# Two transformer layers in one kernel: dt made ahead of the x-projection by a merged weight, and attention's parts stored first

## The reference

```
xz = u @ m_in_w.T;  xc, z = split(xz)
xc = silu(causal_conv4(xc) + conv_b)
x_dbl = xc @ xproj_w.T                        # 8 columns for dt, 16 for B, 16 for C
dt = softplus(x_dbl[..., :8] @ dt_w.T + dt_b) # 256 channels
Bm, Cm = x_dbl[..., 8:24], x_dbl[..., 24:]
h = exp(dt * A) * h + dt * Bm * xc            # a scan over 512 steps, 16 states per channel
y = (sum over states of h * Cm + xc * Dp) * silu(z)
return y @ m_out_w.T
```

## Time and profile before

| | us |
|---|---|
| median of 3 timed runs | 2080.14 (2078.58 to 2081.39) |
| the profiled execution, its own time | 2059.48 |
| its span in the trace | 2057.8 |
| TensorE busy in the span | 1652.5 (80%) |
| VectorE busy | 1350.7 (66%) |
| ScalarE busy | 1003.5 (49%) |
| GpSimd busy | 995.8 (48%) |

### The profile page before, as it was taken

The page is one execution under the profiler, slowest core; times in us unless marked ns, Lnnn a source line. Parts: engine busy times, 40 slices in busy tenths (PEclk is TensorE's granted clock), DMA queues, the critical chain, the costliest instruction groups (busy, mean ns, idle before and its releaser), DMA issues. The chain is left out here.

```text
span 2057.8 us, 23202 instructions
## 1 busy us (share of the span) xinstructions
PE 1652.5 (80%) x7221; PEld 730.4 (35%) x7221; DVE 1350.7 (66%) x1527; ACT 1003.5 (49%) x1638; POOL 995.8 (48%) x524
## 2 busy tenths in 40 slices
PE   7767788888888888875855957698888889879998
PEld 5221222222222222211454744354444445633333
DVE  3079999999999999999552123566565655384444
ACT  3566666676666776674122523154444445441111
POOL 1169999999999999998441153011111000040000
PEclk8878888888888888877957966599999989989999
DMA  3044344434443433333003221422233330100001
GB/s 140 2 104 104 92 103 103 103 93 103 103 103 95 101 90 88 89 87 91 16 30 103 82 67 50 116 59 56 49 77 79 79 79 4 46 0 0 0 0 41
DMA packets 78636, 145.41 MB, mean 71 GB/s; under 512 B 10214, under 2 KB 40782, under 8 KB 76854
## 3 DMA queue, kind: packets, MB, share of 16 engines
q1 hardware_dynamic: 75350, 134.98, 25.8%
q0 software_dynamic: 3216, 9.51, 1.4%
HBM read 87.27 MB, written 23.53 MB: 54 GB/s over the span
## 5 line engine op out<-in xcount | busy, mean ns | idle before, releaser
L574 POOL TENSOR_TENSOR PR<-H,CS 128x1024 f32<-128x1024 f32 x256 | 599.4, 2359 | 75.1 <-DVE H L550 52.8
L550 DVE TENSOR_TENSOR_SCAN H<-DA,X 128x1024 f32<-128x1024 f32 x192 | 431.1, 2273 | 0.0
L456 PE MATMUL psY<-PR,fold 128*64 128x512 f32 x1024 | 341.0, 766 | 4.9 <-POOL PR L574 4.9
L538 DVE TENSOR_TENSOR X<-DU,psB 128x1024 f32<-128x1024 f32 x192 | 235.8, 1228 | 72.9 <-DMA DU<-ab 56.8
L526 ACT ACTIVATE DA<-DT,negA 128x511 f32<-128x511 f32 x384 | 247.6, 709 | 7.3 <-DMA DT<-W 6.4
L1278 ACT ACTIVATE a_PT<-a_psS 128x512 f32<-128x512 f32 x320 | 181.3, 601 | 138.5 <-PE a_psS L1182 134.6
L1325 DVE TENSOR_REDUCE a_MX<-a_psM 128x1 f32<-128x384 f32 (+3 forms) x352 | 205.0, 635 | 47.0 <-PE a_psM L1197 45.5
L1196 PE MATMUL a_psM<-a_kst,a_qst 72*128 72x512 bf16 (+3 forms) x512 | 147.4, 336 | 28.0 <-DMA a_kst<-scratch_k 17.5
L550 DVE TENSOR_TENSOR_SCAN H<-X,XS 128x1024 f32<-128x1024 f32 x64 | 146.2, 2284 | 30.2 <-ACT X L526 30.2
L585 POOL TENSOR_TENSOR XS<-DU,BS 128x1024 f32<-128x1024 f32 x64 | 151.0, 2360 | 0.0
L436 PE MATMUL psB<-ST,sel 96*128 96x512 bf16 x128 | 60.8, 475 | 106.4 <-DVE X L538 106.4
(11 more groups left out here) (258 smaller groups left out, 2733.0 us busy)
## 6 DMA issues: line engine op xcount, KB each, us to landing
CS<-c_rows SPq DMA_DIRECT2D x128, 256.0 KB, 3.8
DT<-W SPq DMA_DIRECT2D x64, 256.0 KB, 4.3
DU<-ab SPq DMA_DIRECT2D x64, 256.0 KB, 4.4
BS<-c_rows SPq DMA_DIRECT2D x64, 256.0 KB, 5.3
scratch_q<-a_partsq SPq DMA_DIRECT2D x24, 384.0 KB, 3.4
a_qst<-scratch_q SPq DMA_DIRECT2D x8, 1152.0 KB
a_kst<-scratch_k SPq DMA_DIRECT2D x24, 384.0 KB
scratch_k<-a_partsk SPq DMA_DIRECT2D x8, 384.0 KB, 4.4
```

Source lines behind the costliest of these rows:

```text
L456: last = nc.tensor.matmul(psY[h * HP:(h + 1) * HP, n % 2 * T:(n % 2 + 1) * T], fold[:, :], chunk(PR[n % 4], h), start=False, stop=n >= NS - 2)
L538: nc.vector.tensor_tensor(both(X[s % 2][:, :]), DU[p][:, at:at + 2, :], psB[:, :].unsqueeze(1).to_broadcast([P, 2, T]), ALU.mult).then_inc ...
L550: nc.vector.tensor_tensor_scan(H[s % 4][:, :], decay, x, 0.0, ALU.mult, ALU.add).then_inc(scan_done, 1)
L574: nc.gpsimd.tensor_tensor(both(PR[s % 4][:, :]), both(H[s % 4][:, :]), CS[q % 2][:, s // 2 % 2, :].unsqueeze(1).to_broadcast([P, 2, T]), A ...
```

## The change

- One matrix of 256 x 256 takes the place of two. In the inputs stage TensorE transposes the eight dt rows of xproj, VectorE copies them, TensorE multiplies them by dt_w, and VectorE copies the result to dtW. dt is then dtW times xc, two matmuls of 128 rows for each half, in place of one matmul of 8 rows on the x-projection's result.
- d0 and d1 come before xp, n1 and n2 in the turn. On TensorE d0 and d1 move to slots 4 and 5, xp to 8, n1 to 9, n2 to 10, c0 to 11 and 12; on ScalarE d0 is in slot 5, d1 in 6, xp in 9, n1 and n2 in 10 and 11, c0 in 13 (it was 12).
- Exp goes into slot 6 and Ln into 7, with a decay between them. They stood together in slot 8.
- GpSimd makes dt in slot 7 (it was 9) and du in slot 11 (it was 10). SyncE sends DT before the store of B and C.
- The prelude's order becomes c0, c1, d0, d1, xp, n1, n2, z0, z1, with Silu in two halves; the z half runs after the first decay.
- In attention SyncE runs `store_parts` before the first `send_maxima` instead of after it.

```diff
 def mamba_inputs_stage(...):
+            @block.vector
+            def _(dve):
+                dve.wait_ge(dtW_step, 1)
+                nc.vector.tensor_copy(xprojT[:, :], dt_ps[0:104, :]).then_inc(dtW_step, 1)
+                dve.wait_ge(dtW_step, 3)
+                nc.vector.tensor_copy(dtW[:, :, :], dtW_ps[:, :, :])
             @block.tensor
             def _(pe):
+                for c in range(NCH):
+                    last = nc.tensor.transpose(dt_ps[0:104, c * P:(c + 1) * P], w("xproj")[:, c * 104:(c + 1) * 104], w("ident"))
+                last.then_inc(dtW_step, 1)
+                pe.wait_ge(dtW_step, 2)
+                for c in range(NCH):
+                    last = nc.tensor.matmul(dtW_ps[:, c, :], xprojT[96:104, c * P:(c + 1) * P], w("dt_w")[96:104, :], start=True, stop=True)
+                last.then_inc(dtW_step, 1)
 def mamba_stage(...):
-        PE_AT = {3: ("mout",), 4: ("xp",), 5: ("n1",), 6: ("n2",), 7: ("d0",), 8: ("d1",),
-                 10: ("c0a",), 11: ("c0b",), 13: ("c1a",), 14: ("c1b",), 16: ("z0",), 17: ("z1",)}
+        PE_AT = {3: ("mout",), 4: ("d0",), 5: ("d1",), 8: ("xp",), 9: ("n1",), 10: ("n2",),
+                 11: ("c0a",), 12: ("c0b",), 13: ("c1a",), 14: ("c1b",), 16: ("z0",), 17: ("z1",)}
...
-                last = nc.tensor.matmul(pp[:, :], w("dt_w")[96:104, n * P:(n + 1) * P], xd[96:104, :], start=True, stop=True)
+                if n == 0:
+                    pe.wait_ge(silu_done, v + 2 if u is not None else 1)
+                for c in range(NCH):
+                    last = nc.tensor.matmul(pp[:, :], dtW[:, c, n * P:(n + 1) * P], chunk(UZ[pv], c), start=c == 0, stop=c == NCH - 1)
...
+            if k == "exp":
+                act.wait_ge(pp_copied, used(u, "d1") + 1)
+                nc.scalar.activation(ab[:, :], ab[:, :], ACT.Exp, scale=-1.0).then_inc(softplus_step, 1)
+                return
+            if k == "ln":
+                act.wait_ge(softplus_step, 2 * v + 1)
+                nc.scalar.activation(ab[:, :], ab[:, :], ACT.Ln, bias=1.0).then_inc(softplus_step, 1)
+                return
...
-                if j == 9 and more:
+                if j == 7 and more:
                     pool_dt(pool, u + 1, 1 - p)
-                if j == 10 and more:
+                if j == 11 and more:
                     pool_du(pool, u + 1, 1 - p)
...
                     if c.more_m:
+                        if c.more_p:
+                            store_parts(sp, c.t + 2, c.p)
                         send_maxima(sp, c.t + 1, 0, c.base + c.use["MA"] + 1, 1 - c.p)
                         if c.more_p:
-                            store_parts(sp, c.t + 2, c.p)
                             sp.wait_ge(S_ready, UNITS_T * c.t + UNITS_T + 1)
                             load_stack(sp, c.t + 2, c.p)
```

More of the change, by code:

```diff
@@ L287, in _, with dt_weights @@
                     (before.pool if before else aside)(pool)
+def dt_weights(W):
+    at = OFF1["wmod0"][0] + NCH * T
+    return W[:, at:at + NCH * NCH * P].rearrange("p (c m) -> p c m", c=NCH)
 def mamba_inputs_stage(nc, W, hT, XP, convW, diagD, sel, fold, nsel):
+    dtW = dt_weights(W)
     w = lambda name: W[:, OFF1[name][0]:OFF1[name][1]]
@@ L462, in act_step @@
             if k == "silu":
-                act.wait_ge(pp_copied, EACH * u + BEFORE if u is not None else used(None, "z1") + 1)
-                if u is not None:
-                    act.wait_ge(fin_done, u + 1)
+                act.wait_ge(pp_copied, EACH * u + BEFORE)
+                act.wait_ge(fin_done, u + 1)
                 nc.scalar.activation(UZ[pv][:, :], pre[:, :], ACT.Silu).then_inc(silu_done, 1)
+                return
+            if k == "silu_u":
+                act.wait_ge(pp_copied, used(None, "c1") + 1)
+                nc.scalar.activation(UZ[0][:, 0:NCH * T], pre[:, 0:NCH * T], ACT.Silu).then_inc(silu_done, 1)
+                return
+            if k == "silu_z":
+                act.wait_ge(pp_copied, used(None, "z1") + 1)
+                nc.scalar.activation(UZ[0][:, NCH * T:], pre[:, NCH * T:], ACT.Silu).then_inc(silu_done, 1)
+                return
+            if k == "exp":
+                act.wait_ge(pp_copied, used(u, "d1") + 1)
+                nc.scalar.activation(ab[:, :], ab[:, :], ACT.Exp, scale=-1.0).then_inc(softplus_step, 1)
+                return
+            if k == "ln":
+                act.wait_ge(softplus_step, 2 * v + 1)
+                nc.scalar.activation(ab[:, :], ab[:, :], ACT.Ln, bias=1.0).then_inc(softplus_step, 1)
                 return
@@ L485, in act_step @@
                 nc.scalar.copy(ST[pv][0:32, :], pp[0:32, :])
-                nc.scalar.copy(xd[0:104, :], pp[0:104, :]).then_inc(pp_copied, 1)
+                nc.scalar.copy(xd[:, :], pp[0:2 * NS, :]).then_inc(pp_copied, 1)
             elif k[0] == "n":
@@ L655, in _ @@
                 pe.sem_inc(Y_done, 6)
-                for k in FIRST[:10]:
+                for k in FIRST[:9]:
                     pe_step(pe, k, None, 0, 0)
-                pe.wait_ge(pp_copied, used(None, "n2") + 1)
                 for s in range(5):
                     pe_spread(pe, s, s, 0, True)
-                    if s < 3:
-                        pe_step(pe, FIRST[10 + s], None, 0, 0)
+                    if s < 4:
+                        pe_step(pe, FIRST[9 + s], None, 0, 0)
                 with pe.Fori(0, B - 1) as i:
@@ L675, in _ @@
             def _(act):
-                for k in FIRST[:10]:
+                for k in FIRST[:9]:
                     act_step(act, k, None, 0, 0)
-                    if k == "z1":
-                        act_step(act, "silu", None, 0, 0)
+                    if k == "c1":
+                        act_step(act, "silu_u", None, 0, 0)
+                    if k == "d1":
+                        act_step(act, "exp", None, 0, 0)
+                        act_step(act, "ln", None, 0, 0)
                 act.wait_ge(dt_loaded, 64)
@@ L682, in _ @@
                     act_da(act, s, s, 0, True)
-                    if 1 <= s < 4:
-                        act_step(act, FIRST[9 + s], None, 0, 0)
+                    if s == 0:
+                        act_step(act, "silu_z", None, 0, 0)
+                    else:
+                        act_step(act, FIRST[8 + s], None, 0, 0)
                 with act.Fori(0, B - 1) as i:
```

37 lines of the change are left out of this document (18 added, 19 removed).

## The result

| | before | after |
|---|---|---|
| median, us | 2080.76 (2078.58 to 2087.53, 4 runs) | 2220.51 (2214.6 to 2223.68, 4 runs) |
| profiled execution, its own time | 2059.48 | 2223.68 |
| its span | 2057.8 | 2222.0 |
| granted clock of TensorE, mean | 0.837 | 0.857 |

The changed kernel takes 1.0662 of the time before, with a 95% interval of 1.0628 to 1.0697: 140 us more. 2257 had been forecast, in a range from 2160 to 2290.

A forecast was written before the change was run, and what follows sets the result against it. VectorE was taken as the bound, with what stands ahead of psB deciding. Turns +182, merged weights +3, start -1, attention -7 gave +177 us; with the 1% from profile to median, 2257, range 2160 to 2290.

The forecast's parts named there:

- rival (a): TensorE's clock stays up in the gaps or returns at once: +94 us, 2174; chance 0.27 together with the mixtures.
- psB decides, by the chain of scan, X, copy, step, psB: State-space turn: steps waiting for a copy behind X delay psB, so VectorE's products of states 8, 12, 16 wait.
- State 8: 6.8 less 0.7: Product of state 8 late by 6.8 us at half clock (3.9 at full), less 0.7 for the clock's return.
- State 12: 3.55: Product of state 12 late by 3.55 us at half clock, 2.2 at full, behind n1 and a psY pair.
- State 16: 6.2 less 0.7: Next unit's first product late by 6.2 us at half clock (3.4 at full), less 0.7 for the clock's return.
- What goes: 2.7: VectorE's old waits per turn, for psB, X in scan 11 and DU, vanish: 2.7 us a turn.
- The last turns: Fifteenth turn, without a c step, +7 us; the last turn, with none of the three steps, nothing.
- GpSimd at no cost: Moving dt behind state 7 and du behind state 11 costs nothing, cover 3 us (0.8 at full clock).
- Merged weights +3, start -1, attention -7: Merging in inputs +3 us (1 to 5), stage start -1 (-9 to +4), attention's earlier parts store -7 (0 to -22).
- Putting the 1% between profile and median on top: Timed median 2080.14 is 1% above the profiled 2059.48; the difference was put on the sum, giving 2257.
- (b): Rival: DU decides, waiting 4.3 us instead of 2.7 before the product of state 16: +22, 2097; chance 0.04.
- (c): Rival: it gets faster, TensorE passing d1 before psB for state 8 is wanted: 2052; chance 0.05.

The follow-up runs named there:

- the experiment: Kernel before with only SyncE's order in attention changed, the parts stored ahead of the row maxima MA: 0.997 (0.9949 to 0.9991) of the kernel before.

## Why the prediction was right, and where it was off

The 2220 measured lie between the forecast of 2257 and rival (a), 2174, and they are the mixture of the two that the prediction names: half clock behind the first two gaps, full clock behind the third. Of the signs that it named, only a clock near 0.5 behind the third gap failed.

*psB decides, by the chain of scan, X, copy, step, psB.* Right, in all three places, and shown: with one copy ahead of X, or the step behind the spread, the wait in that place goes; with the copy moved, although the step stands where it did.

*State 8: 6.8 less 0.7.* 6.63 to 6.67 measured. The 0.7 for the clock's return was wrong: d1 and the whole psY pair ran at half clock. 0.55 a turn too little. The 4.9 us came from one return in the kernel before; the other one in the same turn took some 13 us, from 304.8 to about 318.

*State 12: 3.55.* 3.30 to 3.52 measured. Right.

*State 16: 6.2 less 0.7.* 3.45 measured, the price at full clock. The step that failed is the choice of the clock for all three gaps: I judged it by the length of the gap and took "near 4" us of idleness to be enough for half clock, with rows at 2.55 and 4.66 alone to go by the earlier trace rows. The gap was 3.38 long and the clock stayed at 1.00. The length is no measure of it, since behind the shorter gap of 2.55 the clock had been 0.50; what decides stays open. 2.05 us in 14 turns, 29 us, are four fifths of the 36.5 by which the forecast was high. The 0.55 at state 8 has the other sign and hides a quarter of it in the total. With the first gap filled, this place did run at half clock and cost 4.86.

*What goes: 2.7.* The waits named are gone, but VectorE's closing product also waited 0.3 to 0.4 for psY each turn, 11.1 us in the stage with 5.6 of them at once, and does so no more. Together: 12.5 forecast, less 2.05, plus 0.55, less 0.15 at state 12 and less 0.35 for psY, is 10.5; 10.3 were measured, and 0.2 are not accounted for.

*The last turns.* 7 and 0 forecast, 8.8 and 0.7 measured. In the fifteenth DU came 2.9 us late, not 1, and state 8 cost 6.6, not 6.1.

*GpSimd at no cost.* Right: no wait for DU in the turns that have a c step. The cover of 3 us was thinner than computed, since the third delay was: product 16 starts 16.0 us after product 12, not 18.2, and less the prediction's 15.2 that is 0.8; the copy of c0 ahead of X showed 0.8 to 1.4.

*Merged weights +3, start -1, attention -7.* 3.3 in the trace; 10.3 won and 6.4 given back, so -3.9 for the start; and for attention -3.9 in the trace of the changed kernel, -2 to -10 by the interval of the experiment. All within their bounds.

*The sum.* 142.5 for fourteen turns (the first counted at 8.8 as its own waits give it), 8.8, 0.7, 3.3, -3.9, -3.9: 147.5 on 2059.5, or 1.0716. The two measured ratios are 1.0662 and 1.0698, so the rows account for all of it and for 4 to 11 us too much. The 3 us by which the two executions differ ahead of the inputs stage are not in this sum, and where the excess comes from is not shown.

*Putting the 1% between profile and median on top* was harmless, but its meaning was probably another, not a slower run of everything. The kernel before has medians of 2057 to 2059 in the two sets in which the combine is short and of 2078 in the one in which it is some 15 to 20 us longer. No trace of the kernel before from such a chip was taken, so this is inferred.

*The rivals.* (a) and (b) were each made on the chip and came out at 1.0418 against 1.045 and 1.0067 against 1.008, each with its own waits. (c), that it gets faster, needed psB in time. With du's slot moved too, the kernel had 0.9818 where (c) had 0.987, but that agreement is luck: (c) had 9 us from the start, 22 from attention and nothing from the turns, while here 2.3 us go in each turn (54.6 to 52.3) and 4 to 6 in attention.

## What to carry to other kernels

When one engine's list feeds another in strict order, look up for every moved step which copy it waits for and what that copy is queued behind; here a step was cheap only behind the last urgent instruction of its slot. Do not add up what single stalls cost: here a stall of 6.65 us in each of 15 turns was worth 25 to 58 us of its 100, because the next ones grew. And ask at once for the second path, since here it stood about 1 us behind the first and cost 4.5 to 4.9 when the first was cleared.

## What the runs showed of the hardware

- The length of an idle stretch of TensorE did not tell the clock behind it: 3.38 us were followed by 1.00 in the changed kernel, 3.08 by a mean of 0.65 over 4 us with the first gap filled, and 2.55 by 0.50 in the kernel before. What the engine had done before differed; which part of that decides was not tried.
- Work that is done for the clock alone can pay: 52 useless matmuls a turn made the changed kernel 2.3 to 2.6% faster; 20 in one gap of the three made it no faster.
- Ln between Exps costs ScalarE two table loads of 1.28 us each beside its own 1.06. Where they stand ahead of a decay that is wanted, VectorE waits about 2 us (1.92 to 2.29).
- The combine of the first mixture took 38 to 41 us in the sets of two chips and 56 to 58 in that of a third, whatever the kernel; in the long ones VectorE has waits without a releaser in the profile.
